# Issuing two small SBUF transfers per head pair from ScalarE instead of SyncE in a cross-attention and routed-FFN kernel

## The reference

```
def _L0_xattn_ref(x, context, ln_gamma, ln_beta, w_q, w_kv, w_out, b_out, gate):
    xn = _layernorm(x, ln_gamma, ln_beta)
    q = (xn @ w_q).reshape(B, SQ, NUM_HEADS, DIM_HEAD)
    kv = context @ w_kv
    k, v = jnp.split(kv, 2, axis=-1)
    scores = jnp.einsum('bqhd,bkhd->bhqk', q * SCALE, k)
    attn = jax.nn.softmax(scores, axis=-1)
    out = jnp.einsum('bhqk,bkhd->bqhd', attn, v).reshape(B, SQ, INNER)
    out = out @ w_out + b_out
    return out * jnp.tanh(gate[0])
...
x = x + jnp.tanh(g_xattn[0]) * _L0_xattn_ref(_layernorm(x, axis=-1), ctx_1024, L0_xattn_ln_gamma, L0_xattn_ln_beta, L0_xattn_w_q, L0_xattn_w_kv, L0_xattn_w_out, L0_xattn_b_out, L0_xattn_gate)
x = x + jnp.tanh(g_ffn[0]) * _L0_ffn_ref(_layernorm(x, axis=-1), L0_ffn_gate_w, L0_ffn_w1, L0_ffn_w2)
```

## Time and profile before

| | us |
|---|---|
| median of 3 runs | 587.85 |
| the runs | 586.03, 587.85, 588.67 |
| the profiled execution | 586.77 |
| its span in the profile | 585.0 |
| TensorE busy | 506.5 (87%) |
| VectorE busy | 436.3 (75%) |
| ScalarE busy | 360.5 (62%) |
| GpSimd busy | 338.2 (58%) |

### The profile page before, as it was taken

One profiled execution on the slowest core, in us unless ns is written; L12 is line 12 of the kernel. 1 busy time (PEld: TensorE's weight loads), 2 busy tenths in 40 slices (PEclk: granted clock), 3 DMA queues, 4 the chain that ended last, 5 costly groups with the idle time before them and its releaser, 6 DMA issues.

```text
span 585.0 us, 16296 instructions
## 1 busy us (share of the span) xinstructions
PE 506.5 (87%) x5644; PEld 447.7 (77%) x5644; DVE 436.3 (75%) x814; ACT 360.5 (62%) x671; POOL 338.2 (58%) x207
## 2 busy tenths in 40 slices
PE   4657988799989998999899998999899989985294
PEld 3446877698879887888789887988788879775194
DVE  4577977579886889878987988698869897876112
ACT  3445767467765776667675776577667765762041
POOL 4553568637584657646664666466647565665115
PEclk9877999899999999999999999999999999999588
DMA  7886778847785778757775777677757766750201
GB/s 197 192 220 176 188 190 193 212 99 176 167 203 135 171 162 195 164 129 177 167 177 129 174 166 182 140 176 166 172 130 174 166 154 154 167 149 15 91 4 41
DMA packets 48686, 91.22 MB, mean 156 GB/s; under 512 B 6515, under 2 KB 21539, under 8 KB 48656
## 3 DMA queue, kind: packets, MB, share of 16 engines
q1 hardware_dynamic: 47280, 87.53, 64.9%
q0 software_dynamic: 1376, 3.30, 1.6%
HBM read 10.83 MB, written 5.14 MB: 27 GB/s over the span
## 4 chain that ended last, share of the span: by engine, by line
PE 41%; SPq 27%; DMA 11%; issue 8%; DVE 6%; ACT 4%; POOL 1%; DVEq 0%; POOLq 0%; ACTq 0%
SPq L416 10%; DMA ST<-MROW 8%; SPq L418 7%; PE psS L1107 6%; SPq L428 5%; PE psS L1108 5%; PE psX L1187 4%; PE psM L1083 4%; PE psO L1128 3%; PE psO L1130 2%; PE psO L1129 2%; DVE MX L805 2%; ACT P L662 2%; SPq L433 2%; PE psKQ L1021 2%
## 5 line engine op out<-in xcount | busy, mean ns | idle before, releaser
L558 POOL TENSOR_TENSOR PARTS<-P,PARTS 128x1024 f16<-128x1024 f32 x128 | 274.6, 2146 | 182.9 <-ACT PARTS L706 114.3
L662 ACT ACTIVATE P<-psS 128x512 f32<-128x512 f32 x256 | 146.3, 599 | 62.6 <-PE psS L1108 57.3
L805 DVE TENSOR_REDUCE MX<-psM 128x2 f32<-128x1024 f32 x128 | 155.8, 1217 | 15.9 <-PE psM L1083 15.1
L1107 PE MATMUL psS<-ST 128*128 128x256 f32 x512 | 144.9, 310 | 25.3 <-DMA ST<-MROW 20.4
L1107 PEld LDWEIGHTS psS<-ST 128*128 128x128 f32 x512 | 97.7, 191 | 44.0 <-issue 27.1
L1108 PE MATMUL psS<-ST 128*128 128x256 f32 x512 | 131.0, 283 | 0.0
L1128 PE MATMUL psO<-VH,PARTS 128*128 128x65 f16 x1024 | 108.1, 196 | 2.2 <-POOL PARTS L558 1.6
L1129 PE MATMUL psO<-VL,PARTS 128*128 128x64 f16 x1024 | 106.9, 193 | 0.0
L1130 PE MATMUL psO<-VH,PARTS 128*128 128x65 f16 x1024 | 106.6, 194 | 0.0
L622 ACT ACTIVATE HL<-psKQ 128x768 fp32r<-128x768 f32 x62 | 50.4, 812 | 79.7 <-PE psKQ L1023 76.4
L1108 PEld LDWEIGHTS psS<-ST 128*128 128x128 f32 x512 | 98.4, 192 | 1.0
(11 more groups left out here) (168 smaller groups left out, 818.8 us busy)
## 6 DMA issues: line engine op xcount, KB each, us to landing
ST<-HL SPq DMA_DIRECT2D x128, 384.0 KB, 5.4
ST<-HL SPq DMA_DIRECT2D x128, 192.0 KB, 4.9
ctx_raw<-in_ctx_dram SPq DMA_DIRECT2D x8, 256.0 KB, 4.7
ST<-MROW SPq DMA_DIRECT2D x128, 1.0 KB
w1s<-in_L_ffn_w_dram SPq DMA_DIRECT2D x8, 256.0 KB, 4.7
w2s<-in_L_ffn_w_dram SPq DMA_DIRECT2D x8, 256.0 KB, 3.2
experts_table<-O POOLq DMA_DIRECT2D x2, 645.0 KB, 8.0
PARTS<-experts_table SPq DMA_DIRECT2D x2, 516.0 KB, 4.2
```

The lines of the kernel that those rows point to most:

```text
L558: pool.tensor_tensor(PLO[:, par, h, :], P32[:, h, :], PHI[:, par, h, :], ALU.subtract).then_inc(plo_done, 1)
L662: act.activation(P32[:, h, 512 * (c % 2):512 * (c % 2) + 512], psS[c % 2][:], ACT.Exp, scale=SCALE).then_inc(exp_done, 1)
L805: dve.tensor_reduce(MX[:, hp % 2, h, :], psM[:], AX.X, ALU.max, negate=True).then_inc(max_done, 1)
L1107: pe.matmul(dst, ST[:, buf, h, AK + P * kt:AK + P * kt + P], ST[:, buf, h, AQ:STW], start=True, stop=False)
```

## The change

SyncE's function `max_rows` goes to ScalarE, with the same two DMAs. ScalarE runs it directly behind `max_row`, so after the copy of L632 and before `kq_hi`. It gets one more wait, on `score_psum`, which on SyncE the stack transfers had held already: the place in `ST` must be free. ScalarE also waits for its own copy to be complete (`mrow_done`). SyncE's queue keeps the stacks, loads and stores, and no longer waits for the copy.

```diff
-            def max_rows(b, hp):
-
-                j = b * PAIRS + hp
-                buf, par = hp % BUFS, hp % 2
-                sp.wait_ge(mrow_done, j + 1)
-                for h in range(2):
-                    dst = ST[64:65, buf, h, BQ:BK].bitcast(F32)
-                    sp.dma_start(dst, MROW[QT * h:QT * h + QT, par, :].bitcast(F32)).then_inc(mrow_in[par], 16)
...
-            for hp in range(AHEAD - 1):
+            for hp in range(AHEAD):
                 stacks(0, hp)
-            sp.wait_ge(stack_consts, 1)
-            max_rows(0, 0)
-            stacks(0, AHEAD - 1)
...
-                    if not (is_last(b) and hp + 1 >= PAIRS):
-                        max_rows(*next_pair(b, hp, 1))
...
+            def max_rows(b, hp):
+
+                j = b * PAIRS + hp
+                buf, par = hp % BUFS, hp % 2
+                if not (is_first(b) and hp < BUFS):
+                    act.wait_ge(score_psum, 4 * j - 4 * (BUFS - 1))
+                act.wait_ge(mrow_done, j + 1)
+                for h in range(2):
+                    dst = ST[64:65, buf, h, BQ:BK].bitcast(F32)
+                    act.dma_start(dst, MROW[QT * h:QT * h + QT, par, :].bitcast(F32)).then_inc(mrow_in[par], 16)
...
             max_row(0, 0)
+            act.wait_ge(stack_consts, 1)
+            max_rows(0, 0)
...
                     if not (is_last(b) and hp + 1 >= PAIRS):
                         max_row(*next_pair(b, hp, 1))
+                        max_rows(*next_pair(b, hp, 1))
```

## The result

The changed kernel takes 603.13 us (median of 4 runs, 602.05 to 605.65), the kernel before on the same chip 588.25 us. The ratio is 1.027, with a 95% interval of 1.022 to 1.031: the change makes the kernel 15 us slower, where 15 us faster was forecast. The profiled execution spans 603.9 us; the one of before spans 585.0. These two lie further apart than the medians, 18.9 against 15 us: the one after was the slowest of its four (605.65), the one of before 1.5 under its median.

A forecast was written before the change was run, and what follows sets the result against it. It took TensorE as nearest its limit, idling 25.3 us before first scores, mostly for maxima late through SyncE's issue order. Gains of 5, 2.5, 5 and 2 us made 14.5, rounded to 15, so 573 us; range 562 to 612.

The forecast's parts named there:

- Part 1: SyncE loses two issues a pair; the stack's start gains nothing and nothing waits for it, so 0 us.
- Part 2: Maxima issued earlier, 2.3 and 0.5 us in two pairs, shortening TensorE's wait before L1107; ceiling 25.3 us.
- the sum: Gain over the stretches of the kernel: first batch 5, single wait 2.5, rest of middle 5, last pairs 2; 14.5 us.
- The two pairs that the text read: Pairs 28 and 29, read by timeline: 14.35 us now, 14.0 after, 0.35 gained of TensorE's 0.60 idle.
- the 4.9 us: Idleness before L1107 that the profile gives to small VectorE steps, counted as waiting for the maxima.
- L1107 idle under 8 us: Sign of being right: TensorE's idleness before a pair's first score falls under 8 us from 25.3.
- the second rival: ScalarE's issues stretched to about 1.8 us, 10 us lost against about 10 gained: 588 us (580 to 594), chance 0.20.
- Part 3: ScalarE gains two issues a pair before `kq_hi`, priced at 1.4 us, mostly hidden by its idleness there.
- the cover: ScalarE's idleness before `kq_hi`, waiting for TensorE's projection, 1.23 us a pair on the mean, to hide the issues.
- The upper bound: ScalarE's two issues, held until 6.4 us after the stack's first issue, would take 2.9 us.
- The point of decision: ScalarE becomes the engine that sets the pace from about 1.8 us of issue on.
- The third rival: ScalarE sets the pace, `kq_hi` behind issues of 2.5 to 2.9 us: 620 to 640 us, milder 600 to 610; chance 0.27.

The follow-up runs named there:

- run four: Changed kernel with one 2 KB DMA for both heads' maxima, issued by ScalarE, and two small TensorE transposes a pair instead of one: 569.28 us, ratio 0.968.
- run eight: Changed kernel with the same two ScalarE DMAs, but head 1's issued behind `kq_hi` instead of ahead of it: 568.66 us, ratio 0.965.
- run one: Changed kernel with one more wait on SyncE, so the stack is issued only after ScalarE's copy of the maxima: 603.45 us, ratio 1.024.
- three: Kernel before, all DMAs on SyncE, with each stack issued one place later, behind the maxima it stood ahead of: 658.07 us, ratio 1.115.
- run two: Changed kernel with ScalarE issuing only head 0's maxima, and SyncE head 1's at its place in the kernel before: 576.53 us, ratio 0.980.

## Why the prediction was wrong

**The bound** was read rightly. SyncE's order took part in the end, and TensorE was near its limit: in the runs that free both (four, eight) it is busy 89% of the span.

**Part 1, SyncE's relief at 0,** is not contradicted. Nothing waited for an earlier stack; stacks that come later, though, cost at once (runs one and three).

**Part 2, maxima that leave earlier,** held. The wait for them fell from 20.4 to 5.2 us, and the beginning is 5.7 us shorter, where the sum had 5 for the first batch. Where the issue doesn't hold ScalarE, the kernel gains 12 (run two) and 19 to 20 us (four and eight), and the sum said 15. The two pairs that the text read, 14.35 us with 14.0 forecast, take 14.09 in run eight, so this reading was nearly right. Not in the sum by themselves are the first pairs of the batches, where most of the middle's gain sits. And the 4.9 us that were counted to the wait for the maxima, though the profile puts them down to VectorE, are not of it: 4.5 of the 16.7 us of run eight and 4.1 of the 5.7 of run four are still there. The sign "L1107 idle under 8 us" did not come in the kernel after either (18.6). Two slips of arithmetic change nothing: 11.5 by 0.35 of 0.60 is 6.7 and not 6, and the second rival's turn is 7.50 and not 7.45.

**Part 3, ScalarE's two issues,** is the step that failed: the term of 1.4 us, which was to fit into the idleness before `kq_hi`. The text bounded them by 1.17 and 2.9 us and took 1.4, "because ScalarE's issues enter a queue with no backlog of its own". Measured: 0.58 for the first, mostly 1.3 to 1.9 for the second, and 2.47 us from copy to `kq_hi` in the pair shown. That is 1.24 us over the cover of 1.23, where the forecast had 0.17 over it, so `kq_hi` is late. The reason was right for the first DMA only. The upper bound had been written down with nearly the right mechanism, "if all that held ScalarE" (ScalarE is held until 5.5 and not 6.4 us after the stack's first issue), and the trace of before had the number: taken one by one, SyncE's two issues of the earlier trace rows behind the stack are 1.6 and 0.85 us, and the first of them ends 5.5 us after the stack's first issue, when ScalarE's second one ends now. The prediction had looked at the two together. The short 1.28 us behind the store, which the text took for a sign that the backlog doesn't count, says only that the store had sat out the wait: it was issued 4.13 us after the stack's first and ended 5.81 after it.

The Trainium skill's rule, cited there from Perfetto Trace Analysis, section "DMA Instruction — HWDGE (DVE, Sync)", was the better guide here. It says that two sequencers share the block that generates descriptors, under a lock, and that the profiled duration includes the wait. It names DVE and Sync as the two, not ScalarE. This case agrees in that the second DMA on ScalarE's queue mostly lasts 1.3 to 1.9 us behind SyncE's stack and 0.57 where the stack was issued longer ago; it does not show why the first one of ScalarE, in the middle of the same stack, takes 0.58.

**The cover** of 1.23 us is borne out from both sides: 1.15 us of spare work is hidden, 2.20 us cost 20.4. The point of decision, put at about 1.8 us of issue, lies between these two; no run stands at it.

**The third rival** is what happened, in its milder size. Its signs were named ahead: a wait before `kq_hi` that is gone, and pairs above 7.4 us. The duration of 0.9 us for each issue was named too; it holds for the second of each pair. Its sum was too large. It took a turn of 8.1 us in 48 pairs, 43 us, and 10 us less for the gain. The measured loss of the middle is 23.0 us, in which the middle's own gain is already set off: in batch 3, as an example, five pairs lose 0.2 to 1.1 us, 3.6 together, and three lose nothing. Against run eight, which has the gain and not the hold, batch 3 loses 5.4 us, and that is the rival's six times 0.9. But the first batch loses only 1.7 so, the last 2.4, and the gain to be set off is 19.5 and not 10. In one of the three pairs that lose nothing the copy comes after the moment of release, as the first lines of ScalarE's timeline show. It had a chance of 0.27 against 0.45 for the forecast. By the earlier trace rows, read as above, they should have stood the other way round.

**Open.** The runs show that ScalarE's second issue behind a stack, and SyncE's own fifth, are held until about 5.45 us after the stack's first one. The stack's four issues are nearly as long in every pair, so the moment may as well be counted from a later one of them. The runs don't tell what is held: a lock, a limit on descriptors in a shared block, or the first DMA's own place in it. Nor was an issue from GpSimd tried. Run four loses its waits before the scores almost wholly and run eight keeps 16.7 us of them, at the same time within 1 us. Their lists of waits show where the rest is: TensorE waits 13.2 us for VectorE's rough maxima before the transposes in run four, 1.8 in run eight. Why the one kernel waits here and the other there was not tested.

## What to carry to other kernels

A DMA issue moved to a compute engine costs that engine's time, and that time depends on what the other queues have just been given: read at what moment an issue behind the largest burst is let go, counted from the burst's first issue, and take as the price what is left of that time when the engine reaches its own issue. Compare the price with the idleness in front of the next instruction on that engine. If it doesn't fit, carry less with fewer DMAs, or put one instruction for which others wait ahead of the second issue.

## What the runs showed of the hardware

- An engine's first DMA beside another engine's burst is taken in 0.57 to 0.61 us, even 3.4 us after the burst's first issue, with its fourth under way (kernel after: 265.41 against 262.02 and 264.82). Its second, started 3.5 us or more behind the burst's first issue, is mostly held: 44 of the 51 that took over 1 us end 5.37 to 5.57 us after it (the burst is a stack of four transfers and 1.15 MB). Started 0.44 us behind it, at the burst's beginning, it is not held (0.57 us, run one). The issue of SyncE's own fifth DMA ends at that moment too (264.94 + 1.59 = 266.53, 5.51 us after 261.02, in run two).
- A DMA issue of ScalarE runs beside an activation ahead of it in the program: in run eight it starts 0.07 us after `kq_hi` (257.99 and 257.92), which lasts 0.81. The activation behind an issue waits for its end: in the kernel after, `kq_hi` starts at 267.80, 0.27 us behind the end of the second issue.
